# Memory attention of a decoder layer: four heads to a step, scores in row halves of TensorE, value products one group later

## What is computed

```python
x = x + _L0_xattn_ref(_layernorm(x), ctx_1024, ln_g, ln_b, Wq, Wkv, Wm, Wo, bo)

def _L0_xattn_ref(x, memories, ln_g, ln_b, Wq, Wkv, Wm, Wo, bo):   # HEADS 16, DIM_HEAD 64, INNER 1024
    xn = (x - mu) * rsqrt(var + EPS) * ln_g + ln_b
    q = _split_heads(xn @ Wq)
    kv = xn @ Wkv
    k, v = _split_heads(kv[..., :INNER]), _split_heads(kv[..., INNER:])
    mem = _split_heads(memories @ Wm)
    k, v = concatenate([k, mem], axis=2), concatenate([v, mem], axis=2)
    attn = softmax(einsum('bhid,bhjd->bhij', q, k) * DIM_HEAD ** -0.5)
    return einsum('bhij,bhjd->bhid', attn, v) (heads side by side) @ Wo + bo
```

## Time and profile before

| | |
|---|---|
| time before, median of 3 runs | 3851.46 us (3849.82 to 3857.27) |
| the profiled execution's own time | 3860.68 us |
| its span, first to last instruction | 3858.9 us |
| memory attention: memset of `qx` begins, last addition to X begins | 641.4 us, 2280.4 us |
| mean granted TensorE clock over the span | 0.932 |

### The profile page before, as it was taken

The page is one execution under the profiler, slowest core; times in us unless marked ns, Lnnn a source line. Parts: engine busy times, 40 slices in busy tenths (PEclk is TensorE's granted clock), DMA queues, the critical chain, the costliest instruction groups (busy, mean ns, idle before and its releaser), DMA issues. The chain is left out here.

```text
span 3858.9 us, 96632 instructions
## 1 busy us (share of the span) xinstructions
PE 3457.9 (90%) x26993; PEld 2501.2 (65%) x26993; DVE 2455.5 (64%) x8041; ACT 2429.0 (63%) x8827; POOL 1444.0 (37%) x2160
## 2 busy tenths in 40 slices
PE   8999998999999999999999973188897999996776
PEld 5666665788877777777887752166565666663444
DVE  7888886555555555555555554011665788878997
ACT  6888886666666666666666640032675999982221
POOL 6888885000000000000000012400664777765665
PEclk9999999999999999999999985599998999996666
DMA  4000000000000000000000010122000000000000
GB/s 129 0 0 0 0 0 2 2 2 2 2 2 2 2 2 2 2 2 1 2 2 2 2 66 10 54 81 73 22 17 10 6 5 6 5 4 6 11 11 17
DMA packets 80357, 54.27 MB, mean 14 GB/s; under 512 B 24801, under 2 KB 74413, under 8 KB 80160
## 3 DMA queue, kind: packets, MB, share of 16 engines
q1 hardware_dynamic: 76192, 45.27, 4.1%
q0 software_dynamic: 4096, 8.16, 0.7%
HBM read 32.67 MB, written 20.97 MB: 14 GB/s over the span
## 5 line engine op out<-in xcount | busy, mean ns | idle before, releaser
L135 POOL TENSOR_TENSOR b_ln_var_eps<-b_ln_mean_var,all_eps 128x1 f32<-128x1 f32 x128 | 33.1, 259 | 1476.4 <-DVE b_ln_mean_var L129 1476.4
L681 PE MATMUL b_sc<-b_kT,b_qx 128*128 128x205 f32 x2048 | 485.3, 360 | 1.2 <-ACT b_pr L901 1.2
L901 ACT ACTIVATE b_pr<-b_sc,b_low 128x205 f32<-128x205 f32 x1024 | 431.2, 429 | 68.6 <-DVE b_low L760 64.1
L467 ACT ACTIVATE a_pr<-a_sc,a_low 128x128 f32<-128x128 f32 x1024 | 364.2, 381 | 37.2 <-POOL a_pn L511 26.2
L782 DVE COPY b_prT<-b_tr 128x512 f32<-128x512 f32 x256 | 177.1, 692 | 322.9 <-PE b_tr L693 322.9
L681 PEld LDWEIGHTS b_sc<-b_kT,b_qx 128*128 128x128 f32 x2048 | 330.7, 189 | 78.9 <-issue 77.1
L774 DVE TENSOR_SCALAR b_pn<-b_pr,b_rec 128x205 f32<-128x205 f32 x1024 | 289.2, 325 | 58.8 <-DVE b_rec L769 7.4
L2065 ACT ACTIVATE f_pr<-f_sc,f_low 128x77 f32<-128x77 f32 x1024 | 319.0, 335 | 10.8 <-DVE f_low L1956 2.6
L693 PE MATMUL b_tr<-all_ident,b_pn 128*128 128x128 f32 x2048 | 307.7, 273 | 2.7 <-DVE b_pn L774 2.4
L760 DVE TENSOR_REDUCE b_low<-b_sc 128x2 f32<-128x410 f32 x512 | 295.6, 577 | 19.2 <-PE b_sc L681 19.1
L502 POOL TENSOR_TENSOR a_kx<-a_qk,w_hsel 128x512 f32<-128x512 f32 x256 | 291.7, 1151 | 2.4 <-DVE a_qk L338 2.4
(11 more groups left out here) (290 smaller groups left out, 8982.5 us busy)
## 6 DMA issues: line engine op xcount, KB each, us to landing
scratch_x<-r_zeros SPq DMA_DIRECT2D x12, 512.0 KB, 5.2
e_xr<-scratch_x SPq DMA_DIRECT2D x24, 256.0 KB, 3.0
scratch_y<-e_yr SPq DMA_DIRECT2D x24, 256.0 KB, 2.4
all_X<-in_x SPq DMA_DIRECT2D x8, 512.0 KB, 7.0
e_w<-in_e_w SPq DMA_DIRECT2D x16, 256.0 KB, 3.1
out_x<-all_X SPq DMA_DIRECT2D x8, 512.0 KB, 3.2
w_mask<-in_mask SPq DMA_DIRECT2D x1, 2464.0 KB, 8.9
b_cT<-in_ctxT SPq DMA_DIRECT2D x32, 77.0 KB, 1.9
```

What stands on the lines that cost most here:

```text
L467: op = act.activation(pr[:, u % 2, g], sc[:, u % 2, 128 * g:128 * g + 128], ACT.Exp, bias=low[:, u % 2, g:g + 1], scale=-1.0, accum_out=su ...
L681: last = pe.matmul(sc[:, i % 2, KN * h:KN * h + KN], qx[:, p, 2 * i + h], kT[:, p, i], start=True, stop=True)
L901: op = act.activation(pr[:, i % 2, h, 0:KN], sc[:, i % 2, KN * h:KN * h + KN], ACT.Exp, bias=low[:, i % 2, h:h + 1], scale=-1.0, accum_out ...
```

## The change

- Heads go in four groups j of four heads (two pairs i in each). Their scores use row tiles: head h = 0 of a pair has its queries and keys in partitions 0 to 63 and uses the upper half of the array's rows, h = 1 the lower half, and the two write different PSUM banks. `qx` with its zeros is gone; `q` takes one copy of 128 partitions for a chunk where there were two of 64.
- A step is now: first transpose of group j, chunks (`EARLY`), values of group j - 1, scores of group j + 2, second transpose of group j, chunks (`LATE`).
- `tr` is one bank instead of two, and VectorE makes all copies to `prT`. `sc` has four banks instead of two. `po` and `p_y` share a bank.
- `mv` is no longer multiplied: the memory's keys `ck` are transposed (four 128-column transposes a chunk).
- The second normalisation is folded into the first: GpSimd works out a combined factor from the variance with seven small operations (`both_norms`), and GpSimd adds the bias bo beforehand.
- `xT` is now a chunk, and stands directly ahead of the chunk `q`, 0 where the next sequence is even.

```diff
-        sc = mem.psum("sc", [128, 2, 512])
-        tr = mem.psum("tr", [128, 2, 512])
+        sc = mem.psum("sc", [128, 2, 2, 512])
+        tr = mem.psum("tr", [128, 512])
         pj = mem.psum("pj", [128, 2, 512])
-        po = mem.psum("po", [128, 512])
...
-        SLOT = [[[0, 1], [2, 3], [4], [5], [6], [7, 8], [9, 10], [11]],
-                [[0], [1], [2], [3], [4], [5], [6], [7]]]
+        CHUNKS = [[("mk", 0), ("mk", 1), ("mk", 2), ("mk", 3), ("xT", 0), ("q", 0), ("k", 0), ("q", 1), ("k", 1),
+                   ("mv", 0), ("v", 0), ("v", 1), ("mv", 1)],
+                  [("xT", 0), ("q", 0), ("k", 0), ("q", 1), ("k", 1), ("mv", 0), ("v", 0), ("v", 1), ("mv", 1)]]
+
+        EARLY = [[[0, 1], [3, 4, 5], [7], [10]], [[0], [], [4], []]]
+        LATE = [[[2], [6], [8, 9], [11, 12]], [[1], [2, 3], [5, 6], [7, 8]]]
...
                     if kind == "q" and c == 0:
-                        pe.wait_ge(xT_copied, b + 1)
+                        pe.wait_ge(pj_copied, n)
...
-                        half = wm[:].rearrange("p (c i) d -> p c (i d)", c=2)[:, c]
-                        last = pe.matmul(dst[0:CK], cT[:, p], half, start=True, stop=True)
+                        for t in range(4):
+                            last = pe.transpose(dst[0:CK, 128 * t:128 * t + 128], ck[:, 4 * c + t, p], consts.ident[:])
...
-                    for h in range(2):
-                        last = pe.matmul(sc[:, i % 2, KN * h:KN * h + KN], qx[:, p, 2 * i + h], kT[:, p, i],
-                                         start=True, stop=True)
+                    for i in range(2):
+                        for h in range(2):
+                            r = slice(XD * h, XD * h + XD)
+                            last = pe.matmul(sc[:, j % 2, h, KN * i:KN * i + KN], q[r, p, 2 * j + i],
+                                             kT[r, p, 2 * j + i], start=True, stop=True, tile_position=(XD * h, 0))
...
+                    if due(m):
+                        pe.wait_ge(prT_made, m)
...
+                    for j in range(NJ):
+                        transposes(b, j, 0)
+                        if not last:
+                            for k in EARLY[1 - p][j]:
+                                project(b + 1, 1 - p, k)
+                        if j > 0:
+                            values(b, p, j - 1)
+                        elif not first:
+                            values(b - 1, 1 - p, NJ - 1)
+                        if j < 2:
+                            score(b, p, j + 2)
                         elif not last:
-                            score(b + 1, 1 - p, i + 2 - NP)
-                        transposes(b, i)
...
+                            score(b + 1, 1 - p, j - 2)
+                        transposes(b, j, 1)
                         if not last:
-                            for k in SLOT[1 - p][i]:
+                            for k in LATE[1 - p][j]:
                                 project(b + 1, 1 - p, k)
...
+                        if j == 0 and not first:
+                            project_out(b - 1, 1 - p)
...
+                        copy_probs(b, j, 0)
...
+                        if more:
+                            divide(nb, nj, 0)
...
+                        copy_probs(b, j, 1)
+                        if j < 2:
+                            lowest(b, j + 2)
...
+                        if more:
+                            divide(nb, nj, 1)
...
-                for t in (qx, vm, pr, pn):
+                for t in (vm, pn):
                     dve.memset(t[:], 0.0).then_inc(zeroed, 1)
```

More of the change, by code:

```diff
@@ L710, in values @@
-                    last.then_inc(pv_made, 1)
-                def project_out(b):
-                    pe.wait_ge(oT_made, 2 * b + 2)
-                    if due(b):
-                        pe.wait_ge(y_added, b)
-                    pe.wait_ge(xT_copied, b + 3 if not isinstance(b, int) else min(b + 3, B))
+                        if due(b):
+                            pe.wait_ge(y_added, b)
+                    if due(n):
+                        pe.wait_ge(oT_made, n)
+                    for i in range(2):
+                        for t, v in enumerate((vt, vm)):
+                            for h in range(2):
+                                f = XD * (4 * j + 2 * i + h)
+                                last = pe.matmul(po[XD * h:XD * h + XD, 128 * i:128 * i + 128], v[:, p, f:f + XD],
+                                                 prT[:, j % 2, i, h, t], start=t == 0, stop=t == 1,
+                                                 tile_position=(0, XD * h))
@@ L718, in project_out @@
+                    last.then_inc(pv_made, 1)
+                def project_out(b, p):
+                    pe.wait_ge(oT_made, NJ * b + NJ)
                     for i in range(NP):
-                        last = pe.matmul(p_y, oT[:, i], wo[:, i], start=i == 0, stop=i == NP - 1)
+                        last = pe.matmul(p_y, oT[:, p, i], wo[:, i], start=i == 0, stop=i == NP - 1)
                     last.then_inc(y_made, 1)
@@ new lines, in step @@
+                    for j in range(NJ):
+                        more = j < NJ - 1 or not last
+                        nb, nj = (b, j + 1) if j < NJ - 1 else (b + 1, 0)
+                        copy_probs(b, j, 0)
+                        if j == 1 and ahead:
+                            norm_statistics(dve, ln, X[:, b + 2], b + 2, p)
+                        if more:
+                            divide(nb, nj, 0)
+                        if j == 1 and ahead:
+                            norm_moments(dve, ln, p)
+                        copy_probs(b, j, 1)
+                        if j < 2:
+                            lowest(b, j + 2)
+                        elif not last:
+                            lowest(b + 1, j - 2)
+                        if j == 1 and not last:
+                            move_context_keys(b + 1, 1 - p)
+                        if j == 2 and ahead:
+                            dve.wait_ge(pj_made, chunk_end(b + 1, 1 - p, "xT", 0))
+                            norm_apply(dve, ln, X[:, b + 2], b + 2, p)
+                        if more:
+                            divide(nb, nj, 1)
+                        if j == 0 and not (isinstance(b, int) and b == 0):
@@ L849, in _ @@
                 lowest(0, 1)
-                divide(0, 0)
+                divide(0, 0, 0)
+                divide(0, 0, 1)
                 over_sequences(dve, step)
```

325 lines of the change are left out of this document (140 added, 185 removed).

## The result

| | before | changed |
|---|---|---|
| median | 3854.36 us (4 runs) | 3633.56 us (3626.26 to 3635.92, 4 runs) |
| profiled execution | 3860.68 us | 3633.43 us |
| span | 3858.9 us | 3631.6 us |
| memory attention: first memset to last addition to X | 1639.0 us | 1410.8 us |

The ratio is 0.9423 (95%: 0.9402 to 0.9443). The time lies inside the range (3565 to 3720), 18 us above the forecast of 3616. Between the profiled executions the change is -227, where the sum said -236. The other 9 us are only the scale: the profiled execution of before lay 9 above the median shown then, the one of the changed kernel lies on its median.

What follows compares the result with a forecast made beforehand. TensorE's queue was taken as the bound: 25.28 us per sequence less (a), (b) and (c) is 21.05, plus (e) 21.7. Over 64 sequences that saves 229, with (f) 236, giving 3616 us; range 3565 to 3720.

Steps and rivals of the forecast that it cites:

- (a): Scores: row halves overlap fully, 16 slots of 0.174 instead of 32 records, -2.78 us per sequence.
- (b): TensorE's changes of tiling: four visits of three changes at 0.53 instead of eight at 0.34, -0.60 us per sequence.
- Rival 2: Scores: row halves do not overlap, +178 us, giving 3794 us; chance 0.06.
- (c): The memory's values: eight transposes of 0.109 instead of four records of 0.43, -0.85 us per sequence.
- (e): New TensorE waits that the old order hid: +0.5 for xT and +0.15 for others, +0.65 us per sequence.
- xT trip: Wait for ScalarE's copies ahead of the w_wq product: about 1.0 us every second sequence, +0.5 per sequence.
- (f): Start of the stage: memsets go and the product with w_wq starts near 650 instead of 656.87, -7 us.
- rival 1: VectorE's order: late second copies delay transposes in two of four steps, 1.6 us per sequence, giving 3718; chance 0.11.
- rival 3: Single tr bank: copies always late, up to 1.01 us per transpose block, slower at 4133 us; chance 0.05.
- Rival 4: Memory attention without new waits and with cheap changes of tiling: 21.05 to 20.65 us per sequence, 3549 to 3575; chance 0.08.

Runs made afterwards that it cites:

- run 1: The changed kernel with the scores alone put back on the full array, queries padded with zeros in qx: 3776.25 us, ratio 0.9774 to the kernel before.
- run 4: The changed kernel with xT moved ahead of the third mk chunk where the next sequence is even: 3612.49 us, ratio 0.9352 to the kernel before.
- run 7: The changed kernel with the memory's values made by a product again, using the identity's columns (values not the reference's): 3669.28 us, ratio 0.9504.
- run 8: The changed kernel with xT earlier, the product with Wo ahead of the chunk, and q, 0 behind group 1's second transpose: 3587.7 us, ratio 0.9296.
- run 5: The changed kernel with each group's second copy moved from VectorE to ScalarE, behind the second exponentials: 3633.06 us, ratio 0.9403 to the kernel before.
- run 6: The changed kernel with one unused 128x512 VectorE copy per group, ahead of the second copy: 3635.66 us, ratio 0.9408 to the kernel before.
- run 9: The changed kernel with an unused VectorE copy per group behind the minimum, ahead of the second division: 3639.71 us, ratio 0.9429 to the kernel before.
- run 10: The changed kernel with three unused VectorE copies per group ahead of the second copy: 3645.6 us, ratio 0.9446 to the kernel before.
- run 3: The changed kernel with the scores moved from behind the value products to the head of the step: 3717.39 us, ratio 0.9631 to the kernel before.
- run 2: The changed kernel with the two score loops exchanged, all records of one row half before the other's: 3637.73 us, ratio 0.9425 to the kernel before.

## Why the prediction was right, and where its numbers were off

**The bound.** TensorE's queue set the time before, and it sets it now. Work taken from its queue or put into it came back in the time (runs 1, 4, 7, 8). Work moved off VectorE, or one copy added to it where it had idle time, did not (runs 5, 6). Added work counted only where it made TensorE's next transposes late: 0.19 per two sequences in run 9, 0.43 in run 10.

**(a) Scores, -2.78: right.** Run 1 undoes it. Four slots of 0.174 per group are saved, four groups in a sequence. Rival 2 (no overlap) is out.

**(b) Changes of tiling, -0.60: measured -0.76.** Three changes were priced at 0.15 + 0.19 + 0.19 per group. The last, rows to full array, took 0.15, which leaves 4 x 0.49 = 1.96 instead of 2.12 per sequence. Run 1 gives the 0.15 directly. Run 3 gives 0.15 for the fourth change that it adds, as was forecast.

**(c) The memory's values, -0.85: right** as a price (0.86 and 0.44 a chunk). Run 7 also shows that only 0.67 of it per sequence reaches the time; the rest is waits that the longer chunk would have hidden. The whole time of run 7 shows still less (+36 us, 0.56 per sequence), since the stages behind this one were 8 us shorter.

**(e) Waits, +0.65: measured +0.93. This is the term that was mis-sized.** 21.05 less the 0.16 of (b) is 20.89 without waits, and 21.82 was measured. The xT trip was right (0.46 per sequence where 0.5 was said, and 0.05 more for the uncovered load behind it). The step that failed is "Walking two sequences through by these rows gives about 0.1 for each at most once in two sequences; I take +0.15 per sequence together". The places were the right ones, but not the sizes. Per two sequences, the chunk ahead of a late bank costs 0.22 (1.11 for 0.89), the values behind `residual` 0.25 (0.78 for 0.53; VectorE's addition ends at 1232.03), and the last `mk` ahead of the values 0.10 (run 7). With the small ones, 0.08 ahead of another block of values and some 0.05 at two transposes, this is 0.75, where 0.30 was said. The other 0.19 is in the same timeline: 0.10 is the uncovered load behind xT, 0.06 the xT of the other sequence (0.26 to the values at 1226.25, where 0.20 would do), and 0.02 the transposes behind the late bank (0.46 for 0.44). Run 8 takes 1.47 of the 1.86 per two sequences away; the time follows, 3633.56 to 3587.7. The 0.39 that it leaves is 0.08 at a value chunk, 0.16 at an `mk` and the transposes ahead of it, and 0.15 around an xT. Run 4 takes xT's wait by itself; the other two places of run 8 no run parts.

The two errors, -0.16 and +0.28, partly cancel, which is luck. They make 0.12 per sequence, 64 x 0.12 = 8 us of the 9 by which the profiled executions miss the sum.

**(f) The beginning, -7: right.** First memset to first scores fell from 23.94 (641.40 to 665.34) to 16.36 (640.67 to 657.03), -7.6.

**VectorE's order (rival 1, 0.11; rival 3, 0.05): margins read well for one step, the cost of a late copy wrong.** The prediction read margins of 0.1 for the first copy, with the apply of the norm, and 0.35 for the second. In the tighter of the two steps that follow such an apply (1241.47) they measure 0.27 and 0.29. The other seven have more: 0.59 and 0.54 in the step with the least `EARLY` work, and up to 3.61 and 3.12. The prediction let two of four steps pay; only one of eight is near. The reading took the exponentials to start 1.0 into every step. They start when the minimum is written: at 1208.13, ahead of the step that begins at 1208.53, and at 1215.93, 0.8 into the one that begins at 1215.13. What was missed beside it is what follows from a late copy: the bank is wanted only behind the next block of chunks, and a step that falls behind meets a longer one next. So 0.37 of extra work per group cost nothing (run 6), and 1.09 cost 0.43 in two sequences (run 10), where the rival had 3.2. VectorE has 15.4 us per sequence, where the prediction had 16.6 less a second norm that it did not price. For the rule of the Trainium skill on emptying PSUM (TensorEngine Tiling (Array Packing), Performance Considerations), the trace agrees that VectorE's work did not get shorter with the tiling (14.3 to 15.4 us per sequence). The page's case is a TensorE that tiling has made four times faster, while here two halves overlap; that VectorE is the bottleneck here, runs 5 and 6 refute.

**Rival 4** (3549 to 3575) had the cheaper change of tiling right and the waits wrong. Run 8, at 3587.7, is the nearest to it that a run came by order alone.

## What to carry to other kernels

When half-empty weights are packed into row tiles, count the slots that overlap and subtract the changes of tiling, here 0.15 to 0.19 us each by the spacing of starts: 0.70 us of scores saved per group became 0.54. When a dense queue gets shorter, look at once for the copies that the removed work was covering. Waits gave back a fifth of what was saved here (0.93 of 4.39 us per sequence), and two moved chunks and a moved product regained most of it. A narrow margin on another engine cost little here, because what it made late was wanted at once in one step of eight; put an idle instruction there to measure it rather than price it by reading.

## What was not expected of the hardware

- Row halves overlap although their records are not neighbours in the program: with four records of one half ahead of four of the other, eight records of 205 columns took 0.90 us, as in turn (0.89). The start times in the trace put the first two records of a block 7 ns apart in turn, and 13 ns in run 2; the trace does not name their halves, but two that run together so closely are taken to be of different ones.
- A change from row halves to the full array costs 0.15 us (0.09 to empty it, 0.06 for the first load), less than columns to rows (0.09 and 0.10).
